# A stack of four cross-attention blocks on one core: the second phase's kept x alternates between two tiles, and the next pair's block is laid over both halves

## The reference

```python
x = L0(x, ctx)   # 8 heads of 20; three attentions over 16 rows of the context each; + b_out + x
x = L1(x, ctx)   # layernorm, self-attention (20 heads of 64), + x;
                 # layernorm, cross-attention over all 1500 rows (20 heads of 64), + x;
                 # layernorm, geglu feed-forward of width 640, + x
x = L2(x, ctx)   # hs  = attention of x over rows 0..1495 of the context (8 heads of 20)
                 # ca1 = attention of four projected rows over x; ca2 = attention of ca1 over the last 4 rows
                 # x = (hs + ca2) @ Wout + b_out + x
x = L3(x, ctx)   # as L1, with 20 heads of 8
```

## Time and profile before

| what | before |
| --- | --- |
| median of three runs | 5963.16 us |
| the profiled execution's own time | 5963.19 us |
| its span, first to last instruction | 5961.4 us |
| TensorE matmul busy | 5579.6 us, 94% |
| VectorE, ScalarE, GpSimd busy | 2818.5, 3101.7, 3095.7 us |
| mean granted TensorE clock | 0.961 of 2.4 GHz |
| first phase (to its last take of x) | 61.8 to 2661.5 us |
| second phase, 14 whole pairs | 2794.0 to 3683.4 us |
| third phase, from its second take of x | 3945.2 to 5961.4 us |

### The profile page before, as it was taken

The page is one execution under the profiler, slowest core; times in us unless marked ns, Lnnn a source line. Parts: engine busy times, 40 slices in busy tenths (PEclk is TensorE's granted clock), DMA queues, the critical chain, the costliest instruction groups (busy, mean ns, idle before and its releaser), DMA issues.

```text
span 5961.4 us, 92283 instructions
## 1 busy us (share of the span) xinstructions
PE 5579.6 (94%) x34224; PEld 4580.3 (77%) x34224; DVE 2818.5 (47%) x5171; ACT 3101.7 (52%) x7280; POOL 3095.7 (52%) x3472
## 2 busy tenths in 40 slices
PE   7999999999999999998989999799999999999998
PEld 5777777777777777786767767578888888888887
DVE  2444444444444444443555555255445455545452
ACT  1455555555554555553544544356566656566655
POOL 0445454444544445462555545256666666666665
PEclk8899999999999999997999989689999999999999
DMA  2000000000000000000111111100000000000000
GB/s 56 13 17 17 14 17 17 17 16 17 17 10 17 12 17 17 17 21 15 31 29 29 31 26 29 25 17 24 17 17 20 17 21 20 20 17 20 17 21 12
DMA packets 85964, 119.97 MB, mean 20 GB/s; under 512 B 42814, under 2 KB 65194, under 8 KB 85514
## 3 DMA queue, kind: packets, MB, share of 16 engines
q1 hardware_dynamic: 85514, 114.07, 6.9%
HBM read 109.56 MB, written 4.46 MB: 19 GB/s over the span
## 4 chain that ended last, share of the span: by engine, by line
PE 64%; DVE 18%; ACT 9%; DMA 3%; POOL 3%; issue 3%; ACTq 0%; POOLq 0%; SPq 0%; DVEq 0%
PE ps_c L695 13%; DVE mpiece L1458 8%; PE ps_s L1133 6%; PE ps_s L1134 5%; PE ps_s L1135 5%; PE ps_u L1148 5%; PE ps_c L1076 5%; PE ps_u L1150 4%; PE ps_u L1149 4%; PE ps_c L1094 3%; ACT p_hi L1827 2%; ACT p L1825 2%; POOL p_lo L1614 2%; DVE ctx_hi L1449 2%; DVE uT L1485 2%
## 5 line engine op out<-in xcount | busy, mean ns | idle before, releaser
L1614 POOL TENSOR_TENSOR p_lo<-p,p_hi 125x448 fp32r<-125x448 f32 (+2 forms) x2688 | 2716.5, 1019 | 2320.8 <-ACT p_hi L1827 1652.9
L1825 ACT ACTIVATE p<-ps_s 125x448 f32<-125x448 f32 (+2 forms) x2688 | 1324.7, 493 | 1822.6 <-PE ps_s L1135 1617.5
L1827 ACT ACTIVATE p_hi<-ps_s 125x448 fp32r<-125x448 f32 (+2 forms) x2688 | 1319.1, 491 | 0.0
L1458 DVE TENSOR_REDUCE mpiece<-ps_c 125x1 f32<-125x500 f32 (+1 forms) x1984 | 1226.8, 666 | 92.9 <-PE ps_c L1076 89.8
L1133 PE MATMUL ps_s<-q_hi,ctxT_hi 105*125 105x448 f32 (+3 forms) x2688 | 1005.0, 374 | 51.6 <-DVE q_hi L1468 28.5
L1148 PE MATMUL ps_u<-p_hi,ctx_hi 125*97 125x448 f32 (+2 forms) x2688 | 961.6, 358 | 16.1 <-ACT uT L1815 15.1
L1134 PE MATMUL ps_s<-q_lo,ctxT_hi 96*125 96x448 f32 (+2 forms) x2688 | 926.0, 345 | 0.0
L1135 PE MATMUL ps_s<-q_hi,ctxT_lo 96*125 96x448 f32 (+2 forms) x2688 | 922.0, 343 | 0.0
L1149 PE MATMUL ps_u<-p_hi,ctx_lo 125*96 125x448 f32 (+2 forms) x2688 | 914.7, 340 | 0.0
L1150 PE MATMUL ps_u<-p_lo,ctx_hi 125*97 125x448 f32 (+2 forms) x2688 | 913.8, 340 | 0.0
L1076 PE MATMUL ps_c<-ctxT_hi,q_hi 96*125 96x500 f32 (+1 forms) x2112 | 845.3, 425 | 67.5 <-DVE mpiece L1458 58.5
(11 more groups left out here) (226 smaller groups left out, 5898.4 us busy)
## 6 DMA issues: line engine op xcount, KB each, us to landing
ctx_raw<-in_ctx SPq DMA_DIRECT2D x96, 562.5 KB
pT<-recs SPq DMA_DIRECT2D x32, 490.0 KB, 3.6
w_area<-recs SPq DMA_DIRECT2D x32, 490.0 KB, 3.6
w_area<-recs SPq DMA_DIRECT2D x32, 196.0 KB, 3.9
cs<-in_ctx SPq DMA_DIRECT2D x192, 6.0 KB, 3.2
x_between<-x_out SPq DMA_DIRECT2D x32, 80.0 KB
x_in<-x_between SPq DMA_DIRECT2D x32, 80.0 KB
w_area<-in_L_xattn_wq SPq DMA_DIRECT2D x2, 800.0 KB, 6.0
```

Of the source, the lines that this page charges most:

```text
L1458: z = V.tensor_reduce(mpiece[0:wide, k, r:r + 1], C(0, wide, n % banks(t), 0, PIECE), AX.X, ALU.max)
L1614: P.tensor_tensor(p_lo[0:kp, k % 3, 0:w], p32[0:kp, k % 2, 0:w], p_hi[0:kp, k % RING, 0:w].bitcast(F32), ALU.subtract).then_inc(*sig("pl_r ...
L1825: A(p32[0:kp, k % 2, 0:w], ps_s[0:kp, k % 2, 0:w], ACT.Exp, scale=DH[t.ph] ** -0.5)
L1827: A(p_hi[0:kp, k % RING, 0:w], ps_s[0:kp, k % 2, 0:w], ACT.Exp, scale=DH[t.ph] ** -0.5)\
```

## The change

`x_kept` lets `hand` and `post` use `xn` and `x_post` in turn in the second phase, by the pair's number. So `hand` and the head of `pre` no longer wait for `post`, and stand ahead of it in the lane. That lane now covers the first half from slot 0 to one slot before its end; the lane with `split`, `context` and `maxima` ends three slots before the half's end. The wait for `post`'s add moves from the head of `pre` to its step 14. `RECIP` and `POST` become 10 and 16 in the second phase (13 and 20 before), and the cut of `pre` is after step 11 (9 before). The tables change in all three phases: in the first, more room ahead of steps 8, 27, 30 and 35 of `pre`, ahead of `queries`, and ahead of step 6 of `post`; in the third, ahead of step 7 of `pre` and of `queries`. The `pre` of the third phase's first pair starts at slot 20 of the second phase's last half instead of 26, which was behind its end.

```diff
@@ -191,6 +191,11 @@
         hT = sb("hT", [HF, 2, 2, S])
         xn = sb("xn", [128, D])
         xnF = xn
+
+        def x_kept(t):
+
+            return xn if t.ph == 1 and t.it % 2 == 0 else x_post
+
         stats = sb("stats", [128, 6])
         mv = sb("mv", [128, 2])
         ve = sb("ve", [128, 1])
@@ -395,22 +400,22 @@
 
 
         PARTS = {
-            "pre": ((40, 3, {4: 1, 7: 0.5, 8: 3, 10: 1.5, 14: 1.5, 16: 3, 18: 2, 22: 2, 27: 2.5, 30: 1.5, 34: 1, 35: 0.5, 37: 1,
-                             38: 1.5, 39: 2, 40: 4.5}), (29, 3.5, {5: 2, 15: 1.5, 22: 0.5, 23: 2}), (20, 2.5, {2: 3, 6: 1.5, 7: 0.5, 9: 2, 11: 0.5, 13: 1, 15: 1, 19: 2, 20: 1})),
-            "queries": ((7, 1, {1: 2, 7: 3}), (3, 3, {1: 1}), (7, 1, {1: 2, 7: 2})),
+            "pre": ((40, 3, {4: 1, 7: 0.5, 8: 4, 10: 1.5, 14: 1.5, 16: 3, 18: 2, 22: 2, 27: 3, 30: 2, 34: 1, 35: 1.5, 37: 1,
+                             38: 1.5, 39: 2, 40: 4.5}), (29, 3.5, {5: 2.5, 15: 1.5, 22: 0.5, 23: 2}), (20, 2.5, {2: 3, 6: 1.5, 7: 1.2, 9: 2, 11: 0.5, 13: 1, 15: 1, 19: 2, 20: 1})),
+            "queries": ((7, 1, {1: 5, 7: 3}), (3, 3, {1: 1}), (7, 1, {1: 5, 7: 2})),
             "split": ((4, 0.5, {}), (2, 0.5, {}), (4, 0.5, {})),
             "context": ((5, 1, {5: 6}), (4, 4, {}), (5, 1.5, {5: 3})),
             "maxima": ((31, 2.25, {}), (16, 3, {}), (31, 1.75, {})),
-            "post": ((15, 3, {1: 1, 6: 1, 14: 1}), (2, 1.5, {1: 1}), (15, 3, {1: 0.5, 6: 1.5})),
+            "post": ((15, 3, {1: 1, 6: 2, 14: 1}), (2, 1.5, {1: 1}), (15, 3, {1: 0.5, 6: 1.5})),
             "hand": ((1, 1, {}), (1, 1, {}), (1, 1, {})),
         }
 
         LEAD = {"split": 4}
-        CUT = (18, 9, 3)
+        CUT = (18, 11, 3)
         LAST_NORM = (38, None, 18)
 
-        RECIP = 13
-        POST = 20
+        RECIP = (13, 10, 13)
+        POST = (20, 16, 20)
         APART = (4, 2, 4)
         TAIL = 4
 
@@ -524,7 +529,8 @@
                     end += [pre_a]
                 if t.ph == 1:
 
-                    weave(main(t, 0, first=first), lane(parts), lane(end, POST), *norm)
+                    end = end if first else end[1:] + end[:1]
+                    weave(main(t, 0, first=first), lane(parts, 0.0, TAIL - 1), lane(end, 0.0, 1), *norm)
                 else:
                     weave(main(t, 0, first=first), lane(parts + end), *norm)
                 lanes = []
@@ -534,7 +540,7 @@
                 elif not last:
                     lanes = [lane(before(t + 1, pre_b), 0.0, TAIL)]
                 elif t.ph < 2:
-                    lanes = [lane([part("pre", side.pre, At(t.ph + 1, 0, ahead=True))], POST + 6.0)]
+                    lanes = [lane([part("pre", side.pre, At(t.ph + 1, 0, ahead=True))], POST[t.ph] + (4.0 if t.ph else 6.0))]
                 weave(main(t, 1, last=last), *lanes, apart(side.normalise(t, 0)))
 
             for ph in range(3):
@@ -804,7 +810,7 @@
 
                         if t.ph != 1:
                             pe.wait_ge(*got("mr_ready", t, 0))
-                        pe.wait_ge(*got("xp_ready", t, -per("xp_ready", t)))
+                            pe.wait_ge(*got("xp_ready", t, -per("xp_ready", t)))
                     if t.ph == 0:
                         yield from side.pre_0(t)
                     elif t.ph == 1:
@@ -947,6 +953,8 @@
                     yield 12
                     side.out_slots(t, 0, 4, vb0, 20, 1)
                     yield 14
+                    if not t.ahead:
+                        pe.wait_ge(*got("xp_ready", t, -1))
                     side.out_T(t, 0, 0, 0)
                     yield 16
 
@@ -1474,11 +1482,11 @@
                 def normalise(t, b):
 
                     tiles = t.heads // 2
-                    yield RECIP
+                    yield RECIP[t.ph]
                     dve.wait_ge(*got("su_loaded", t, 16 * (b + 1)))
                     V.reciprocal(srec[:, 0:tiles], srec[:, 0:tiles]).then_inc(*sig("rec_ready"))
                     for g, (h0, n) in enumerate(t.groups):
-                        yield POST - 1 + (APART[t.ph] if b else 2) * g
+                        yield POST[t.ph] - 1 + (APART[t.ph] if b else 2) * g
                         if g == 0:
                             dve.wait_ge(*got("rb_loaded", t, 16 * (b + 1)))
                         u = uT[0:DC + 1, h0:h0 + n, b, 0:T]
@@ -1490,9 +1498,9 @@
                 def hand(t):
 
                     yield 1
-                    dve.wait_ge(*got("xp_ready", t, 0))
+                    dve.wait_ge(*got("xp_ready", t, -1 if t.ph == 1 and t.it else 0))
                     dve.wait_ge(*got("xm_ready", t, per("xm_ready", t)))
-                    V.tensor_copy(x_post[:, :], x_mid[:, :]).then_inc(*sig("x_handed"))
+                    V.tensor_copy(x_kept(t)[:, :], x_mid[:, :]).then_inc(*sig("x_handed"))
 
                 @staticmethod
                 def add_post(t, n):
@@ -1502,7 +1510,7 @@
                     final = n + 1 == per("xp_ready", t)
                     if final:
                         dve.wait_ge(*got("x_saved", t, 0))
-                    V.tensor_tensor((x_out if final else x_post)[:, :], x_post[:, :], side_banks(t)(0, 128, 0, 0, D), ALU.add)\
+                    V.tensor_tensor((x_out if final else x_post)[:, :], x_kept(t)[:, :], side_banks(t)(0, 128, 0, 0, D), ALU.add)\
                         .then_inc(*sig("xp_ready"))
 
                 @staticmethod
```

## The result

The changed kernel takes 5889.47 us (median of 5887.77, 5888.23, 5890.70 and 5903.04) where the kernel before takes 5963.07: the ratio is 0.9882, with a 95% interval of 0.9868 to 0.9895. That is 73.6 us less; 85 were forecast (5878), and the range was 5832 to 5942. The profiled execution took 5887.77 us, its span is 5886.0.

What follows compares the result with a forecast made beforehand. TensorE was taken to bound all three phases, through its work, its stalls and what the clock takes. Savings of 63, 10 and 12 us by phase sum to 85, giving 5878 us from 5963.2; the 8-in-10 range was 5832 to 5942.

Steps and rivals of the forecast that it cites:

- Second phase, 63 us: Second phase: pairs fall from 63.5 to 59.3 us, 4.2 us less, over about 15 pairs.
- Stalls that go, 4.4 us a pair: Second phase: spreading the head of pre removes TensorE's waits between links, for q_hi and for uT; 4.4 us a pair.
- The third context group behind `kvb`, 2.0 us: Second phase: TensorE's third context transposes wait for ctxT_lo, queued behind kvb on VectorE; adds 2.0 us, bounds 0 to 3.3.
- Denser maxima, 0.7 us: Second phase: softmax and uT multiply now stand among VectorE's maxima reductions; adds 0.7 us a pair, between 0 and 2.5.
- SyncE issues the same transfers in the same order: SyncE's queue: transfer order unchanged, counted among what costs nothing.
- Clock 0.97, 0.7 us a pair: Second phase: pairs run at a clock of 0.97, costing 0.7 us more than at 1.00.
- Where the clock fell before: Second phase before the change: clock at 0.51 for 9.8 us right behind four close stalls, costing 4 us in that pair.
- First phase, 10 us: First phase: later queries and moved steps shorten TensorE's waits; net 0.65 us a pair over 15 pairs, 10 us.
- Third phase, 12 us: Third phase: the 1.01 us wait for hT goes, denser maxima return 0.2; 0.8 us a pair over 15 pairs.
- the clock still falls: Rival, second phase: stalls shrink by 1.7 us a pair but clock stays 0.93; 48 us saved, 5915 us; chance 0.20.
- VectorE keeps up: Rival, second phase: none of the 2.7 us of new stalls comes; 126 us saved, 5837 us; chance 0.12.
- The slower rival: VectorE's queue holds TensorE: 7.3 us of stalls come, 4.4 go, clock falls every pair; 40 us slower, 6003 us; chance 0.08.

Runs made afterwards that it cites:

- three_edits: Changed kernel with x and cs loads issued first, the uT multiply two slots later, the second kvb multiply behind the three ctxT_lo; 5861.2 us.
- packed_20: Changed kernel with the lane of hand, the block's head and post starting at slot 20 of the second phase's first half again; 5971.0 us.
- first_old: three_edits with the first phase's table rows (the block, queries, post) as before the change; 5862.2 us.
- second_only: Changed kernel with the tables of the first and third phase as before the change; 5899.0 us.
- blocks_later: Changed kernel with vb_s and both kvb multiplies of the second phase behind the three ctxT_lo on VectorE; 5959.9 us.

## Why the prediction was right, and where it was not

**Second phase, 63 us: 63.3.** The sum is right in its end, less so in its terms.
- *Stalls that go, 4.4 us a pair.* By the lists of waits 4.6: `q_hi` 22.5 us over the 14 pairs before, `uT` ahead of L1148 13.7, `kvb` 10.9, the rest 16.6, all gone. (The text ahead of the sum counts six stalls; the earlier trace rows has seven, and the sum rightly leaves out the 0.70 of `mpiece`, which stays.)
- *The third context group behind `kvb`, 2.0 us.* Over-sized: 0.63. VectorE's side was right, 2.9 us from the start of `pT` to the end of `kvb` for the 3.0 reckoned; but TensorE came to the transposes 3.0 us after that start (2889.38 to 2892.34), not 2.0. That `kvb` moves to where GpSimd works and grows by it was right: its median goes from 684 ns to 992, between 675 and 1318 in the changed kernel. three_edits, where the wait is gone with one of the passes, shows it to be this term's. The Trainium skill, "SBUF — State Buffer", section "Who interferes with whom", has a VectorE instruction with two inputs in SBUF contend with a GpSimd one that reads SBUF. The trace agrees in kind; the median grows by 45%, and some of the multiplies do not grow at all.
- *Denser maxima, 0.7 us.* 19.7 us instead of 9.8 over 14 pairs: 0.71.
- *Not in the sum:* `cs`, 1.24 us a pair, which I had only among the things that would make the forecast wrong; L701's wait for `xT`, 0.33; L1084's for `ctxT_lo`, 0.25. The step that failed is "SyncE issues the same transfers in the same order", put among what costs nothing: the order was the same and the need came 20 slots sooner. In all 3.2 us came, not 2.7.
- *Clock 0.97, 0.7 us a pair.* It was 1.00 in each of the 14 pairs, and the 0.7 was not spent. It offsets the stalls that were missing in the sum.
- *Where the clock fell before.* The prediction has it fall right behind the four stalls, for the 9.8 us of the earlier trace rows. It fell sooner and for longer, ahead of the longest stall, which ended at 3244.59:

```profile
3240.60:3254.30 13.70, 12.13 (x53) 9.05 (x54) 3.78 (x8) 4.07 (x8) 3.07 (x3) 0.50 0.00 0
```

Three short stalls among small matmuls came before it (0.31, 0.38 and 0.74 us), and the same stalls stand in the pair from 3049.23, whose clock is 1.00. So the stall for `q_hi` did not bring this fall about.

So the pair came to 59.06 for 59.3 us by two errors of about half a microsecond against each other. The phase's sum is lucky too: 4.2 us for 15 pairs were reckoned, and 4.46 for 14 came, with ends that nearly cancel, 19.9 us won at the start and 19.1 lost at the end, neither of which the prediction had. packed_20 has little of either (130.6 and 267.4 us), so the place of the lane moves them.

**First phase, 10 us: 5.8 in the profile, nothing that holds.** The pairs take 160.3 to 160.8 us with the new rows in ten runs and 160.3 to 160.5 with the old in three; the phase's last take comes at 2655.7 to 2664.7 us with the new and at 2656.1 to 2661.5 with the old; and first_old puts the difference at 1 us. The 5.8 us lie within that scatter. The signs that were named came, the wait for `hT` at 0.33 us a pair and a new one of `post` for `q_hi`, 0.69. The step that failed is the net of 0.65 us a pair. Of it, `queries` behind a block was priced at the block, 0.62 us, and is worth 2.0; and "the other steps move by one block past work that has no wait there" left out what they cost, as much.

**Third phase, 12 us: 6.4**, and 6.6 between second_only and the changed kernel. With the new rows twelve runs take 2007 to 2013 us from the phase's second take on, with the old two take 2016, so there is a gain, between 3 and 9 us. The wait for `hT` went nearly whole (14.5 us over 14 pairs, 0.2 left). The maxima took 0.29 us a pair of that (18.5 for 14.4 us), not 0.2. The step that failed is a term that the sum does not have: the busy time rose by 3.9 us. At least in part that is the clock. It stays up through the first 14 pairs of the phase before and in second_only, and in the changed kernel it falls to half in four short stretches, here one, with TensorE busy throughout:

```profile
4537.60:4541.00 3.40, 3.40 (x11) 2.82 (x10) 1.00 (x3) 0.98 (x2) 1.17 (x2) 0.50 0.00 0
```

Other runs with the new rows have two to six such stretches there. What in these rows brings them about was not tried.

**The rivals.** That the clock still falls is what packed_20 shows for the old place of the block, and is not what the new one does in the second phase. The Trainium skill, "TensorE: Matmul & The Clock Gate", section "A second HAM failure mode: psum-queue depth-cycling", has frequent short idles as enough for the clock to swing: the changed kernel does not agree, with some 90 waits over 14 pairs, 3.9 us a pair, at 1.00; packed_20, with as much idle time (4.2 us a pair) but close together, does. That VectorE keeps up did not hold: 3.2 us of stalls came. The slower rival didn't hold either, but blocks_later shows it to be real: with one piece of 2.7 us in VectorE's queue, in another place, 4.9 us of stalls a pair come, the clock falls in most pairs, and the whole gain is gone. The point that the rival named was 4.4 us.

## What to carry to other kernels

Where TensorE is the bound, price a stall twice: by its length, and by what the clock does behind it; here several short ones in a row among small matmuls, or in most pairs one of two microseconds, cost more than the same time spread over a half. When a step moves ahead, ask of every transfer it reads when it is issued, not only whether the order stays: the load that had 20 slots to spare has none. And of a table that moves many steps, try the rows one at a time: here one was worth 2.0 us a pair beside the old rows, and with the others new as well nothing was left of it.
